# First stage without an inner barrier, weights behind activations and a buffer of their own for expert rows, in a two-layer vision tower on one Trainium2 core

## The reference, cut to what matters

```python
concat = jnp.concatenate((x, lu, ru, ld, rd), axis=1)      # image and 4 shifts by 4 pixels, zero padded
normed = (concat - mean) * rsqrt(var + 1e-7) * gamma + beta   # moments over all of concat, per image
h = conv(normed, W, stride=8) + b                          # -> (128, 169, 128)

xh = layernorm(h)
dist = sqrt(max(|xh|^2 + |p|^2 - 2 xh.p, 0))               # 256 positions p
attn = softmax(scales / (dist + 0.1))
h = h + (attn @ values) @ W_out.T + b_out
h = h + fp8_matmul(layernorm(h), L0_ffn_weight)            # one scale over all tokens
h = h + softmax(xn @ xn.T * SCALE) @ xn                    # xn = layernorm(h), per image

x = layernorm(h)                                           # router, 2 shared and 64 routed experts
p, i = top_k(softmax(x @ router_w.T + bias), 6);  p = p / (sum(p) + 1e-9)
shared = mean over 2 of  (silu(x @ g.T) * (x @ u.T)) @ d.T
expert e: its tokens in order, at most C each:  gate * (silu(x @ wg.T) * (x @ wu.T)) @ wd.T
h = h + shared + sum of the token's experts
```

## Time and profile before

| | us |
|---|---|
| median of 3 runs | 4096.03 (4090.68 to 4097.14) |
| the profiled execution, its own time | 4103.54 |
| its span in the trace | 4101.7 |
| busy: PE, DVE, ACT, POOL | 2888.1, 2655.3, 1512.4, 2720.8 |
| mean granted TensorE clock, share of full speed | 0.678 |

### The profile page before, as it was taken

The page is one execution under the profiler, slowest core; times in us unless marked ns, Lnnn a source line. Parts: engine busy times, 40 slices in busy tenths (PEclk is TensorE's granted clock), DMA queues, the critical chain, the costliest instruction groups (busy, mean ns, idle before and its releaser), DMA issues. The chain is left out here.

```text
span 4101.7 us, 75982 instructions
## 1 busy us (share of the span) xinstructions
PE 2888.1 (70%) x14869; PEld 2249.8 (55%) x14870; DVE 2655.3 (65%) x10164; ACT 1512.4 (37%) x3699; POOL 2720.8 (66%) x4427
## 2 busy tenths in 40 slices
PE   2988888727777777777767752687777777767770
PEld 2767777614544445454544531576676666666660
DVE  4588888846888888888778761344444444466664
ACT  2566666613232323323223211333433344333330
POOL 1355555400687777777757886588888888887881
PEclk7699999855555555555555556677878888877675
DMA  3555555321233333333323224544444444489867
GB/s 158 173 194 189 196 185 186 138 79 29 93 120 106 118 104 116 102 105 93 97 69 93 91 79 117 153 139 140 142 141 138 139 142 134 134 261 290 263 175 256
DMA packets 427082, 582.16 MB, mean 142 GB/s; under 512 B 64858, under 2 KB 345594, under 8 KB 415444
## 3 DMA queue, kind: packets, MB, share of 16 engines
q1 hardware_dynamic: 343668, 418.11, 33.7%
q0 software_dynamic: 83232, 162.29, 11.7%
HBM read 299.55 MB, written 306.56 MB: 148 GB/s over the span
## 5 line engine op out<-in xcount | busy, mean ns | idle before, releaser
L991 POOL DMA_INDIRECT xed<-xr,idxs x1014 | 1002.4, 989 | 528.0 <-POOL pace L996 188.9
L1003 POOL DMA_INDIRECT ytk<-yo,idxy x1080 | 1078.7, 999 | 297.5 <-POOL pace L1008 207.5
L1242 PE MATMUL wide<-wdt,hT 64*128 x2160 | 374.3, 323 | 360.4 <-DVE hT L1720 359.6
L1702 DVE TENSOR_TENSOR idxy<-xr 128x1 int32<-128x1 f32 x1080 | 148.2, 163 | 643.7 <-DMA ytk<-yo,idxy 640.9
L1242 PEld LDWEIGHTS wide<-wdt,hT 64*128 64x128 f32 x2160 | 314.3, 221 | 416.3 <-issue 413.7
L1378 ACT ACTIVATE yo<-wide,gd 128x128 f32<-128x128 f32 x1080 | 307.8, 368 | 633.7 <-PE wide L1242 615.9
L1224 PE MATMUL bank<-wgu,xeT 128*128 x2160 | 388.7, 340 | 0.0
L1224 PEld LDWEIGHTS bank<-wgu,xeT 128*128 128x128 f32 x2160 | 369.6, 258 | 1.5
L537 POOL TENSOR_TENSOR lnr<-rr,scb 128x1024 f32<-128x1024 f32 (+1 forms) x43 | 125.0, 2907 | 354.3 <-ACT rr L631 354.3
L1151 PE MATMUL wide<-xn,e 128*128 128x128 f32 (+3 forms) x1024 | 324.1, 449 | 0.0
L526 POOL TENSOR_TENSOR weff<-w,gam 128x640 f32<-128x640 f32 x169 | 260.7, 1571 | 86.3 <-POOLq L294 77.0
(11 more groups left out here) (312 smaller groups left out, 5918.6 us busy)
## 6 DMA issues: line engine op xcount, KB each, us to landing
xr<-xed SPq DMA_DIRECT2D x1080, 113.0 KB
ytk<-zeros SPq DMA_DIRECT2D x42, 1536.0 KB, 9.4
yg<-ytk SPq DMA_DIRECT2D x42, 1536.0 KB
xs<-in_xcol SPq DMA_DIRECT2D x42, 1280.0 KB
ytk<-yo,idxy POOLq DMA_INDIRECT x1080
xed<-xr,idxs POOLq DMA_INDIRECT x1014
H<-in_ximg SPq DMA_DIRECT2D x4, 2704.0 KB, 18.1
h1d<-H SPq DMA_DIRECT2D x42, 256.0 KB, 2.0
```

What stands on the lines that cost most here:

```text
L991: p.indirect_dma_start(xed[:, :], bass.IndirectOffsetOnAxis(ap=idxs[:, slot, j, k:k + 1], axis=0), xr[:, slot, j, :], None, bounds_check=Z ...
L1003: p.indirect_dma_start(ytk[:, :], bass.IndirectOffsetOnAxis(ap=idxy[:, slot, j:j + 1], axis=0), yo[:, slot, j, :], None, bounds_check=128 ...
L1242: last = pe.matmul(eO[slot % 2][:, j * D:(j + 1) * D], hT[:, slot % 2, j, :], wdt[:, bass.ds(e, 1), :].rearrange("p o f -> p (o f)"), star ...
```

## The change

- `front` is one block. SP issues the loads of the first two groups of patches right behind the weights. GpSimd starts to fold as soon as the weights are in. `gbx` has its own semaphore `gb_in`.
- The moments come from one pass: the first image quarter's mean is the shift (`part[:, 60:61]`), ScalarE squares quarters, edges and corners with that shift while VectorE sums, and the result is corrected by the shift. ScalarE loads the table for roots first.
- TensorE does the row terms of a group in one product of 512 columns, and the positions' squares in one product for two tiles.
- `d2`, `lnr`, `rr`, `lg` and `eT` are views of one tile `big`, in which the squares are also written.
- In `back` the first activations are loaded at once, the weights behind them by ScalarE's queue. The factors 0.5 and 0.25 go into two products that VectorE does anyway (one of them now SCALAR_TENSOR_TENSOR instead of TENSOR_TENSOR, as the other).
- `LATE` is 6 instead of 7.
- `xin` has its own memory. SP begins with the experts' rows when the tables are there and the scatters of the first 30 groups have landed; it waits for the others only before group Q0.

The diff, cut to its core:

```diff
-        with nc.Block() as block:
-            @block.sync
-            def _(sp):
...
+        def statistics(v):
...
+            for i in range(4):
+                v.wait_ge(s_img[i], 16)
+                link(v.tensor_reduce(part[:, i:i + 1], H[:, i * w:(i + 1) * w], AX.X, ALU.add))
+                if i == 0:
+                    v.tensor_scalar(part[:, 60:61], part[:, 0:1], -1.0 / w, None, ALU.mult).then_inc(s_sh, 1)
+                    v.wait_ge(s_sh, 1)
...
+            v.wait_ge(s_sq, 12)
+            weigh(v, link, 16, part[:, 41:42])
+            link(v.scalar_tensor_tensor(part[:, 43:44], part[:, 42:43], NPAD, part[:, 41:42], ALU.mult, ALU.add))
+            v.scalar_tensor_tensor(part[:, 44:45], part[:, 43:44], 1.0 / NPIX, part[:, 46:47], ALU.mult, ALU.subtract)\
+                .then_inc(s_var, 1)
...
+        def squares(a):
...
+            a.wait_ge(s_sh, 1)
+            for i in range(4):
+                a.wait_ge(s_img[i], 16)
+                a.activation(big[:, 0:w], H[:, i * w:(i + 1) * w], ACT.Square, bias=part[:, 60:61],
+                             accum_out=part[:, 16 + i:17 + i]).then_inc(s_sq, 1)
+                a.wait_ge(s_sq, i + 1)
+            for i, view in enumerate(EDGES + CORNERS):
...
+                for g in range(2):
+                    load_x(g, g, 0)
+                store_rows(sp)
+                for g in range(2):
+                    load_gb(g, g, 0)
+                store_squares(sp)
                 sp.wait_ge(s_zero, 1)
-                pipeline(sp, 0, GA, [(0, load), (2, clear), (5, store)])
+                pipeline(sp, 0, GA, [(0, load_x), (0, load_gb), (2, clear), (5, store)], begin=2)
...
+                def conv_gb(g, slot, rnd):
+
+                    nj = tiles_of(g)
+                    pe.wait_ge(gb_in[slot], 16 * (rnd + 1))
+                    pe.matmul(psY[slot][:, 0:nj * D], mstdT[:, :], gbx[:, slot, 0:nj * D], start=False, stop=True)\
+                        .then_inc(conv_done, 1)
...
-    xin = xr
+    xin = sb("xin", [128, ES, TG, XW])
...
-    LATE = 7
+    LATE = 6
...
+            p.memset(h1s[:, :, :, :], 0.0).then_inc(n["s_h1"], 1)
+            p.memset(xe[:, :], 1.0).then_inc(n["s_xe"], 1)
...
             sp.wait_ge(n["tab_ready"], 2)
-            scattered_up_to(GR)
+            sp.wait_ge(n["s_zr"], 16)
+            scattered_up_to(C1)
...
             sp.wait_ge(n["tail_z"], 16 * NE)
+            scattered_up_to(GR)
...
-            v.wait_ge(n["s_wt"], WEIGHTS)
-            v.tensor_scalar(wdt[:, :, :], wdt[:, :, :], 0.5, None, ALU.mult).then_inc(n["s_half"], 1)
-            v.tensor_scalar(sdt[:, :], sdt[:, :], 0.25, None, ALU.mult).then_inc(n["s_half"], 1)
-            v.wait_ge(n["s_c"], 3)
+            v.wait_ge(n["s_c"], 2)
```

More of the change, by code:

```diff
@@ L282, in front @@
         s_sq = sem("s_sq")
+        s_sh = sem("s_sh")
         s_var = sem("s_var")
@@ new lines, in constants @@
+        def constants(g):
+            g.memset(c["ident"][:, :], 0.0).then_inc(s_const, 1)
+            g.memset(c["before"][:, :], 0.0).then_inc(s_const, 1)
+            g.memset(c["ones"][:, :], 1.0).then_inc(s_const, 1)
+            g.memset(c["onesb"][:, :], 1.0).then_inc(s_const, 1)
+            g.memset(c["eps_ln"][:, :], LN_EPS).then_inc(s_const, 1)
+            g.memset(c["tenth"][:, :], 0.1).then_inc(s_const, 1)
+            g.memset(eps_tok[:, :], TOK_EPS).then_inc(s_const, 1)
+            g.memset(zeros[:, :], 0.0).then_inc(s_zero, 1)
+            g.wait_ge(s_const, 7)
+            g.affine_select(out=ident[:, :], in_=ident[:, :], compare_op=ALU.not_equal, fill=1.0, base=0,
+                            pattern=[[-1, 128]], channel_multiplier=1).then_inc(s_fix, 1)
+            g.affine_select(out=c["before"][:, :], in_=c["before"][:, :], compare_op=ALU.is_ge, fill=1.0,
+                            base=0, pattern=[[-1, 128]], channel_multiplier=1).then_inc(s_fix, 1)
+            g.wait_ge(s_fix, 2)
+            g.tensor_copy(c["identb"][:, :], ident[:, :]).then_inc(s_fix, 1)
+            g.tensor_copy(c["beforeb"][:, :], c["before"][:, :]).then_inc(s_fix, 1)
+            g.wait_ge(s_fix, 4)
@@ new lines, in small_products @@
+        def small_products(pe):
+            pe.wait_ge(s_w, 160)
+            pe.wait_ge(s_const, 7)
+            pe.wait_ge(s_fix, 4)
+            for half, (p0, n) in enumerate(((0, 128), (128, T - 128))):
+                for q, src in enumerate((gam, bet)):
+                    dst = wide[0][0:n, (2 * half + q) * D:(2 * half + q + 1) * D]
+                    for k in range(NCTX):
+                        last = pe.matmul(dst, src[:, p0:p0 + n, k], w5[:, k, :], start=(k == 0),
+                                         stop=(k == NCTX - 1 and q == 0))
+                    if q == 1:
+                        last = pe.matmul(dst, ones[0:1, 0:n], tokb[:, :], start=False, stop=True)
+            last.then_inc(s_gb, 1)
+            for a in range(2):
+                dst = wide[0][:, 512 + a * D:512 + (a + 1) * D]
+                pe.matmul(dst, valt[:, a * 128:(a + 1) * 128], wot[:, :], start=True, stop=False)
+                last = pe.matmul(dst, ones[0:1, :], bout[:, :], start=False, stop=True)
+            last.then_inc(s_v2, 1)
@@ L449, in front, with turn_moments, position_squares @@
+        def turn_moments(pe):
+            pe.wait_ge(s_mstd, 2)
+            pe.transpose(bank[2][0:2, 0:128], mstd[:, :], ident[:, :]).then_inc(s_mT, 1)
+        def position_squares(pe):
+            pe.wait_ge(s_psq, 2)
+            pe.matmul(wide[1][0:1, 0:NN], ones[:, 0:1], possq[:, :], start=True, stop=True).then_inc(s_psq, 1)
         xs_in = [sem(f"xs_in{i}") for i in range(2)]
+        gb_in = [sem(f"gb_in{i}") for i in range(2)]
         h1_out = [sem(f"h1_out{i}") for i in range(2)]
@@ L493, in _, with load_x @@
             def _(sp):
-                def load(g, slot, rnd):
+                begin_sp(sp)
+                def load_x(g, slot, rnd):
                     nj = tiles_of(g)
```

303 lines of the change are left out of this document (131 added, 172 removed).

## The result

The changed kernel takes 3948.74 us (median of 4 runs, 3941.15 to 3956.19), the kernel before 4096.59 (median of 4, 4090.68 to 4098.34): a ratio of 0.9641, 95% interval 0.9621 to 0.9662. The prediction was 3940 with a range of 3922 to 3983. The profiled execution took 3956.19 with a span of 3954.3, so the spans differ by 147.4 us, where the sum said 156.

What follows compares the result with a forecast made beforehand. GpSimd's indirect DMAs were taken to set the expert stage's pace, with other limits ahead of it. Gains of 63.6 + 28.6 + 15.4 + 48.5 = 156 us off the median 4096.03 gave 3940 us, range 3922 to 3983.

Steps and rivals of the forecast that it cites:

- First stage, 63.6 us: Start of the first stage: earlier moments and group 0's products beside them bring the third `dist2` 63.6 us earlier; bounds 49 to 67.
- the 17 that I had named as a sign of being wrong: First-stage loop: an interval of `dist2` over 17 us would show the forecast wrong; a regular 16.5 was expected.
- the missing idle time before group 0: First products: group 0's follow the small ones without today's idle time, so first `dist2` near full speed's 63, taken as 65.
- Row terms and squares in one product, 0: First-stage loop: merging takes about 1.4 us a group off TensorE, which waits anyway, so 0 gained.
- Start of the second part, 28.6: Second part's first statistics: weights loaded behind activations let them start at 864.2 instead of 892.82, 28.6 us gained.
- 866 less the shift: Second part's start: ScalarE's first root later than 866 us, less the shift, would show the forecast wrong.
- The factors cost nothing: Second part: factors moved into products cost nothing, since both forms read and write the same elements.
- LATE, 15.4: Router starts one step of pairs earlier, moving GpSimd's first scatter and unbroken stretch by 15.4 us; bounds 7.7 to 15.4.
- Own buffer, 48.5: Before the experts: row loads and zero writes run beside scatters, removing gaps of 18.25 and 31.27; about 48.5 us, lower bound 17.
- rival 2: Expert rows come no earlier in effect: SP's 61.2 us list misses the 63, or loads slow GpSimd; 3971 us, chance 0.14.
- The weights beside later loads: Second part: loads for pairs 2 and 3 land later beside the weights, changing nothing unless they take over 15 us.
- Rival 3: First-stage loop: more idle time lowers TensorE's clock until it sets the loop, up to 8.9 us a group; 4296 us, chance 0.04.

Runs made afterwards that it cites:

- Late squares: Changed kernel with the mean itself as the shift, so ScalarE's squares start only when VectorE has all sums: 5159.62 us, on a slower chip.
- split run: Changed kernel with row terms for each tile apart and the positions' squares for each tile apart: 3946.58 us.

## Why the prediction was right, point by point

- *First stage, 63.6 us: right (62.9), with one wrong reason in it.* Root at 46.55 (I said 45.5), first distances at 65.2 (65), third at 98.3 (97.5). The second interval is 17.1 us, over the 17 that I had named as a sign of being wrong, but it is the only one; the 40 behind it are 16.49 in the mean. Late squares show that the moments carry it one for one. I had put the full clock down to the missing idle time before group 0. The run with late squares has such idle time and still is at full speed at 84.1. What held the kernel before at 0.50 for 78 us was its many products with 2 and 3 rows after a start at half: with them merged and nothing else altered, 19.7 us go. Whether their number or their place between the large ones counts, and whether it is the row terms or the squares, was not told apart. So the 65 came out right partly by luck, as the reason given for it does not hold alone.
- *Row terms and squares in one product, 0: right in this kernel only.* With the early start, 0 for their number (split run); in the kernel before, 19.7 us. The two parts overlap there: the merging alone frees the start from the long stretch at half clock, and so does the early start with the row terms split but kept together, so their worths don't add. Whether the early start does it with row terms between the large products stays open.
- *Start of the second part, 28.6: 26.9.* The step held. The missing 1.7 lies in GpSimd's index tables: the first one starts 10.7 us behind the memset of `h1s` instead of 8.3 (idle for 9.08 instead of 6.90), and 0.7 of these 2.5 come back ahead of the memset. That idle time differs between executions, 7.35 to 9.25 us in the other runs of the changed kernel's kind, by a cause not looked into. ScalarE's first root, at 804.69, is later than "866 less the shift" (866 - 62.9 = 803.1), which I had named as a sign of being wrong. But what it waited for is VectorE's `xe`, behind the late statistics; ScalarE's seven loads were out at 800.3, as the prediction had it. The weights' order alone is worth 18 to 19. The factors cost nothing, as said: the product with `h3s` has a median of 679 ns before and 680 after.
- *LATE, 15.4: 14 to 17* over several profiles, 15.3 at the first scatter of the profiled execution, but 9.5 at its last, which alone is most of the distance from 156 to 147.4.
- *Own buffer, 48.5: 49.2,* and 49.2 again with the wait put back. It is nothing in the two runs on other chips, where the tables aren't ready ahead of the last scatter. The prediction named that cover but not that it hangs on GpSimd's being late, and its sizes were wrong: it had 63 us for a list of 61.2. Measured, the tables are ready 52.3 us ahead of the last scatter, and the list takes 64.1 us, from 2367.3 to 2431.4, so it ends 12.6 us behind the last scatter. That is the condition of rival 2, and it came true. It cost next to nothing; the prediction's argument against that rival, that the rows of group 8 may come some 10 us late without harm, fits this, but no run tests it. In the three kernels of the first set with the wait in its late place, 1.5 to 1.8 us of waiting are left in the first twenty spreads. The term was right with less to spare than the prediction thought.
- *The weights beside later loads.* The third pair's activations were issued at 812.05, beside the weights, and used at 826.74 without a wait, so it changed nothing, as said. There was little to spare: in the run with the small tables behind, they were issued at 809.98, and VectorE waited 2.61 us for them, until 827.39.
- *Rival 3.* The mix did become slower on average, 391 ns a pass against 369, and its wait of some 3 us recurs; the granted clock over the 40 intervals is 0.87 in the mean, against 0.90 before. The intervals stayed at 16.49, since TensorE isn't the bound. The Trainium skill (TensorE: Matmul & The Clock Gate, section HAM oscillation) says that such a wait costs clock each round; the trace agrees in that, and the loop's time shows that it costs nothing here.
- The last gap: 3940 was off the median, and the runs gave 3948.74; the sum was 8.6 too large on the profiles, of which 5.9 are LATE's term in that execution, 1.7 the index tables and 1.1 the stretch behind the twentieth spread, by a cause not looked into.

No run of the first set beat the changed kernel by more than its runs differ (3946.58 against 3948.74). The changed kernel itself did not run on the two other chips. The two runs nearest to it there, group 0's products behind the moments and the small tables behind the first steps, take 103 and 88 us less than the kernel before on their chips (5135.05 and 5162.96), so 45 to 60 us of the 148 are missing there; 49 would be the own buffer's.

## What to carry to other kernels

Price a part in the kernel that the other parts leave behind, and ask which two of them cure the same stretch. A transfer hidden behind an engine's backlog is worth what that backlog is: read the time between what allows the transfer and the end of the backlog (57 us here, -14 elsewhere). And where TensorE sits at half clock while it is busy without a break, as here for 78 us, try merging its small products first.

## What the runs showed of the hardware

- On two of the chips GpSimd was idle for 3.95 us, put down to issue, ahead of every second group of spreads (the first row of the run with half the pauses); that is once for each turn of the program's loop, which does two groups. Idle times of 3 to 4.5 us before a spread came 113 to 126 times in each run there, 444 to 491 us in sum, and never in the six other profiles. From the last scatter to the last sum it took 2035 to 2048 us there, against 1581 to 1583 (SP waiting for all scatters) and 1530 to 1533 (not waiting) in those six, so these idle times are nearly the whole of what the expert stage lost. The braid was longer too, by causes not looked into, and the kernel before took 28% longer as a whole. The loops of the first stage were not touched (16.5 us a group). The cause of the idle times is open.
- Four profiles of kernels that are alike between the first statistics and the last scatter differ by up to 8 us there (1607.9 to 1615.8). A single pair of profiles can't price a part of 15 us by that stretch; six did.
- While GpSimd folded (35.14 to 44.90), four VectorE instructions on one element a partition took 0.5 to 1.18 us; one of the same form right after the last of them took 0.16. All four read two tensors; those with one, in the same time, took 0.15 to 0.16. They stand on the way to the root, which came 1 us later than predicted: ScalarE had its squares done at 41.8, and VectorE turned to them at 45.14. What they cost at the end was not measured.

```profile
43.73 1.18 DVE L370 TENSOR_TENSOR part<-part,mstd 128x1 f32<-128x1 f32 x1
44.94 0.16 DVE L371 TENSOR_TENSOR part<-part 128x1 f32<-128x1 f32 x1
```
